# One signal for four message products, and one GpSimd wait for four gathered slots

## The chip, the cores and the metric

The kernel runs on one core of a Trainium2 chip. The metric is the device time of one launch in microseconds (us), as the median of several runs of the same program. The core has five engines that run at the same time and meet only through semaphores: TensorE (PE in the profile), VectorE (DVE), ScalarE (ACT), GpSimd (POOL) and SyncE (SP), which here only starts transfers.

## The reference, cut to what matters

A graph of 6250 nodes with 256 features and 200,000 edges, sorted by destination, goes through two graph convolutions, a linear attention block and a small mixture of experts:

```python
def _gcn_conv(x, edge_index, edge_weight, W, b):
    ...
    norm = dis[row] * ew * dis[col]
    h = x @ W.T
    msg = h[row] * norm[:, None]
    out = jax.ops.segment_sum(msg, col, num_segments=n)
    return out + b

def _block(x, edge_index, edge_weight, g, bln, W, b):
    h = _layer_norm(x, g, bln)
    h = _gcn_conv(h, edge_index, edge_weight, W, b)
    h = jax.nn.relu(h)
    return x + h
...
x = x + _L0_gnn_ref(xn, edge_index, edge_weight, ...) + _L0_mix_ref(xn[None], ...)[0]
x = x + _L0_ffn_ref(_layernorm(x, axis=-1)[None], ...)[0]
```

For each of the two convolutions every edge needs the row of its source node. The sum over the edges of a node is what the message products below compute.

## The kernel before, in words

The nodes are cut into 49 windows of 128 (`W`), the edges into 1563 chunks of 128 (`NCH`), 32 chunks to a window (`CH`). Each layer of the graph network goes once over the windows. The first layer's pass also computes the attention block of the same window, and the second layer's pass computes the eight experts, in fp16 halves.

A window uses 36 chunks (`USES`): its own 32 and two more at either side (`SIDE`). One use is one message product on TensorE (in `messages`): a 128x128 matrix `ss` that scatters 128 edges, times the 128x256 tile `gs` of gathered source rows, added up in PSUM bank 0 (`acc`). An fp32 product stands as two records in the trace. The products go in groups of four (`U`), one group `k` after the other with the window's other matmuls written out by hand between them (`window1`, `window2`).

Three engines feed this:
- GpSimd gathers a chunk with one indirect DMA into one of the 32 slots of `gs` (`gathers`, 3126 of them in two layers, written out one by one). Slot `n` of the next window may be overwritten once use `n + 2` of this window has been multiplied, so each gather waits on the semaphore `main_used`.
- VectorE builds the matrices `ss` four at a time into a ring of 18 (`scatter_group`, L1098). It waits on `main_used` too, for a value that lies in steps of four.
- TensorE waits on `main_set` for the `ss` of a group and on `main_in0` to `main_in31` for the gathered slots. Each product raises `main_used` by 1, and the last one of a short window by what is missing to 36. It starts at 18, the size of the ring.

TensorE raises many other semaphores, always attached to a matmul, in the order of its program. In a window of the first layer these are 11 beside the 36 of `main_used`: `self_used`, `xn1_tp`, `q_ps`, `nd_ps`, `z1_tp`, `msg_tp`, `h7_ps`, `m_ps`, `mn_tp`, `hh_ps`, `y1_ps`. In a window of the second layer they are 22: `hid_ps` and `y_ps` for each of eight experts, and `x2_tp`, `p_ps`, `z3_tp`, `g_ps`, `mt_ps`, `b2_ps`. After the fp16 matmuls of `hidden` raise `hid_ps`, ScalarE applies the gelu (L732) and copies (L735), VectorE makes the low half (L1222), and only then can TensorE do `expert_out` of that expert.

## Time and profile before

| | us |
|---|---|
| median of 3 runs | 5193.85 (5193.22 to 5195.35) |
| the profiled execution, its own time | 5195.25 |
| its span, first to last instruction | 5193.5 |
| TensorE busy | 3896.0 (75%) |
| GpSimd busy | 3080.2 (59%) |
| VectorE busy | 2524.4 (49%) |
| ScalarE busy | 1187.1 (23%) |

The span is shared by a preparation up to 261 us, the first layer's windows up to 2640 us, and the second layer's up to the end. Busy times are sums over the whole span; what a change is worth has to be read inside a window.

### The profile page before, as it was taken

Reading aid. Unit: us, or ns where it says so; the run is one execution under the profiler, and the core shown is the slowest. Engines: PE = TensorE matmul, PEld = TensorE weight load, DVE = VectorE, ACT = ScalarE, POOL = GpSimd, SP = SyncE. Lnnn points to the kernel's source line nnn. Section 1 sums busy time; section 2 is a strip of 40 time slices with the busy share of each in tenths; the row PEclk is TensorE's granted clock in tenths of the full one; section 3 lists DMA queues with packets and bytes.
Section 4 is the critical chain, followed back from the end, with each engine's and each line's share of the span. In section 5 each row is a group of like instructions: output and inputs, shape, how many; then the busy total and the mean of one; then the engine's idle time right before and its main releaser. Section 6 shows DMA issues by size and latency. Waiting matters only on the chain.

```text
span 5193.5 us, 89964 instructions
## 1 busy us (share of the span) xinstructions
PE 3896.0 (75%) x27204; PEld 3252.7 (63%) x27205; DVE 2524.4 (49%) x8946; ACT 1187.1 (23%) x3161; POOL 3080.2 (59%) x3315
## 2 busy tenths in 40 slices
PE   6847666766766766676658888888888888888888
PEld 4735555555555555555547777776777777777777
DVE  8734444444444444444434554454554554454554
ACT  3500000000000000000013333333333333333334
POOL 3266666666666666666645666666665666566662
PEclk9968877788888888888879999999999999999999
DMA  3333333333333333333323333333333333333331
GB/s 135 129 108 110 108 110 114 108 108 112 109 107 113 111 109 109 113 110 108 113 74 94 94 94 92 95 95 91 97 93 93 93 95 96 92 94 93 93 94 42
DMA packets 269256, 525.71 MB, mean 101 GB/s; under 512 B 62088, under 2 KB 168080, under 8 KB 269200
## 3 DMA queue, kind: packets, MB, share of 16 engines
q0 software_dynamic: 150144, 410.19, 27.0%
q1 hardware_dynamic: 119056, 114.93, 6.7%
q8 instruction: 16, 0.26, 0.0%
q14 instruction: 40, 0.33, 0.0%
HBM read 471.66 MB, written 53.22 MB: 101 GB/s over the span
## 4 chain that ended last, share of the span: by engine, by line
PE 31%; another core or an unknown queue 28%; issue 22%; ACT 10%; DVE 7%; SPq 1%; DVEq 1%; DMA 0%; ACTq 0%; POOL 0%; POOLq 0%
PE bank L1320 30%; ACT bank L732 5%; DVE ss L1098 2%; PE bank L1342 2%; ACT L732 1%; ACT L715 1%; ACT w L735 1%; DVE w L1222 1%; DVE rstd L752 1%; DVE rstd L751 0%; ACT hT L700 0%; DVE rstd L753 0%; DVE u L769 0%; DVEq L1098 0%
## 5 line engine op out<-in xcount | busy, mean ns | idle before, releaser
L571 POOL DMA_INDIRECT gs<-h_d,src_row x3126 | 2996.8, 959 | 1866.1 <-PE bank L1320 881.6
L1320 PE MATMUL bank<-gs,ss 128*128 128x256 f32 x7028 | 1857.2, 414 | 31.2 <-issue 15.2
L1320 PEld LDWEIGHTS bank<-gs,ss 128*128 128x128 f32 x7028 | 1431.2, 211 | 264.0 <-issue 55.3
L1098 DVE TENSOR_SCALAR ss<-iw,dst_all,ew_all 128x128 f32<-128x128 f32 x3514 | 988.8, 357 | 760.6 <-PE bank L1320 549.2
L1320 PE MATMUL bank<-experts,w 128*128 128x256 f16 x4848 | 605.8, 277 | 289.7 <-DVE w L1222 286.3
L1222 DVE SCALAR_TENSOR_TENSOR w<-bank,w 128x512 f16<-128x512 f32 x404 | 278.9, 690 | 1000.1 <-ACT w L735 923.8
L1320 PE MATMUL bank<-w,experts 128*128 128x128 f16 x9696 | 641.0, 220 | 126.1 <-issue 115.4
L732 ACT ACTIVATE bank<-bank,eb1c 128x128 f32<-128x128 f32 x1616 | 450.2, 341 | 1184.6 <-remote 1100.2
L1320 PEld LDWEIGHTS bank<-experts,w 128*128 128x128 f16 x4848 | 458.5, 99 | 391.3 <-issue 320.4
L1320 PEld LDWEIGHTS bank<-w,experts 128*128 128x128 f16 x9696 | 575.1, 98 | 185.5 <-issue 158.9
L1342 PE MATMUL bank<-ident,u 128*128 128x128 f32 x596 | 147.5, 336 | 497.6 <-DVE u L769 370.9
L1342 PEld LDWEIGHTS bank<-ident,u 128*128 128x128 f32 x596 | 81.4, 163 | 587.1 <-DVE u L769 389.3
L1216 DVE SCALAR_TENSOR_TENSOR u<-bank,mask_c,u 128x256 f32<-128x256 f32 x404 | 193.5, 479 | 106.9 <-PE bank L1320 86.7
L735 ACT ACTIVATE w<-bank 128x512 f16<-128x512 f32 x404 | 241.3, 597 | 12.8
L684 ACT ACTIVATE t_a<-t_a 128x256 f32<-128x256 f32 x49 | 20.4, 417 | 637.1 <-issue 470.8
L1320 PE MATMUL bank<-kvx,t_b 128*128 128x132 f32 x196 | 42.3, 347 | 144.6 <-issue 131.4
L1320 PE MATMUL bank<-xT,w 128*128 128x128 f32 x784 | 134.3, 299 | 17.9 <-ACT nT L696 10.2
L696 ACT COPY nT<-bank 128x256 f32<-128x256 f32 x49 | 18.2, 372 | 553.4 <-PE bank L1342 436.1
L700 ACT ACTIVATE hT<-bank,w1bias 128x128 f32<-128x128 f32 x196 | 56.0, 368 | 382.4 <-PE bank L1320 270.9
L1320 PEld LDWEIGHTS bank<-xT,w 128*128 128x128 f32 x784 | 124.5, 218 | 26.2 <-issue 19.7
L1320 PEld LDWEIGHTS bank<-kvx,t_b 128*128 128x128 f32 x196 | 31.1, 225 | 164.3 <-issue 149.1
L1320 PE MATMUL bank<-nT,w 128*128 128x128 f32 x784 | 127.2, 287 | 2.6 <-issue 2.6
(272 smaller groups left out, 3085.0 us busy)
## 6 DMA issues: line engine op xcount, KB each, us to landing
gs<-h_d,src_row POOLq DMA_INDIRECT x3126
hself<-self_d SPq DMA_DIRECT2D x100, 128.0 KB
ew_in<-in_eW SPq DMA_DIRECT2D x49, 168.0 KB
out<-u SPq DMA_DIRECT2D x51, 128.0 KB
u<-xn_d SPq DMA_DIRECT2D x50, 128.0 KB
h_d<-u SPq DMA_DIRECT2D x50, 128.0 KB
self_d<-u SPq DMA_DIRECT2D x50, 128.0 KB
u<-x_d SPq DMA_DIRECT2D x50, 128.0 KB
```

Source lines behind the costliest of these rows:

```text
L571: pool.indirect_dma_start(gs[:, n, :], None, table[:, :], bass.IndirectOffsetOnAxis(ap=src_row[:, c:c + 1], axis=0), element_offset=P * D) ...
L684: act.activation(t_a[1][:, :], t_a[0][:, :], ACT.Exp).then_inc(s["q_exp"], 1)
L700: act.activation(hT[0][:, j, :], bank[6][:, j * P:(j + 1) * P], ACT.Relu, bias=w1bias[:, j:j + 1]).then_inc(s["hr_done"], 1)
L715: act.copy(xT[:, :, :], half(1)).then_inc(s["x2T_set"], 1)
L732: act.activation(hid[e % 2][:, j, :], hid[e % 2][:, j, :], ACT.Gelu, scale=1.0 / (Z_UP * W_UP), bias=eb1c[:, e, j:j + 1]).then_inc(s["gelu ...
L735: act.activation(hT_part[e % 2][0][:, :, :], hid[e % 2], ACT.Copy, scale=H_UP).then_inc(s["h_high"], 1)
L752: ch.link(dve.tensor_tensor(t, t, minus_half, ALU.mult))
L1098: m = dve.tensor_scalar(ss[:, u % S_SLOTS, :], iw[:, :], dst_all[:, c], ew_all[:, c], ALU.is_equal, ALU.mult)
L1216: dve.scalar_tensor_tensor(out=u8[:, :], in0=wide((7, 5)[e % 2]), scalar=mask_c[:, e:e + 1], in1=u8[:, :], op0=ALU.mult, op1=ALU.add).then ...
L1222: dve.scalar_tensor_tensor(out=hT_part[e % 2][1][:, :, :], in0=hid[e % 2], scalar=H_UP, in1=hT_part[e % 2][0][:, :, :], op0=ALU.mult, op1= ...
L1320: return pe.matmul(out_ap, lhsT, rhs, start=first, stop=last, **kw)
L1342: m = pe.transpose(half(b)[:, k, :], src[:, k * P:(k + 1) * P], ident[:, :])
```

## The change

The four products of a group no longer raise `main_used` one by one: the last product of the group raises it by 4 (or by what is missing to 36). GpSimd waits for whole groups: a window's 32 gathers hold 9 waits where they held 32. VectorE's waits keep their values.

```diff
@@ -51,6 +51,7 @@
+assert SIDE < U and CH % U == 0
@@ -564,10 +565,10 @@
                     g, n = layer * W + c // CH, c % CH
-                    if n >= CH - SIDE:
-                        pool.wait_ge(s["main_used"], g * USES + (n - (CH - SIDE)) + 1 + S_SLOTS)
-                    elif g:
-                        pool.wait_ge(s["main_used"], (g - 1) * USES + n + SIDE + 1 + S_SLOTS)
+                    if n == CH - SIDE:
+                        pool.wait_ge(s["main_used"], g * USES + U + S_SLOTS)
+                    elif g and n < CH - SIDE and (n == 0 or (n + SIDE) % U == 0):
+                        pool.wait_ge(s["main_used"], (g - 1) * USES + (n + SIDE) // U * U + U + S_SLOTS)
@@ -1441,7 +1442,7 @@
                     m = mm(acc, ss[:, u % S_SLOTS, :], gs[:, n, :], layer == 1 and u == 0, True, skip_group_check=True)
-                    m.then_inc(s["main_used"], 1 if u + 1 < uses else USES - u)
+                m.then_inc(s["main_used"], U if k * U + U < uses else USES - k * U)
```

No instruction moves. On GpSimd, at the start of the first layer's gathers, the program before reads as follows (`table1` and `tab_set` belong to the preparation, `over_links` to a rare correction step, `table2` is the start of the second layer):

```order
L571 DMA gs<-h_d,src_row 128x256 [waits table1,tab_set]
L571 DMA gs<-h_d,src_row 128x256 x3
...
L571 DMA gs<-h_d,src_row 128x256 x26
L571 DMA gs<-h_d,src_row 128x256 [waits main_used] x1533
L571 DMA gs<-h_d,src_row 128x256 [waits main_used,table2]
```

The changed program has at the same place, for the chunks 4 to 49 of the first layer:

```order
L572 DMA gs<-h_d,src_row 128x256 x26
L572 DMA gs<-h_d,src_row 128x256 [waits main_used]
L572 DMA gs<-h_d,src_row 128x256
L572 DMA gs<-h_d,src_row 128x256 [waits main_used]
L572 DMA gs<-h_d,src_row 128x256
L572 DMA gs<-h_d,src_row 128x256 [waits main_used]
L572 DMA gs<-h_d,src_row 128x256 x3
L572 DMA gs<-h_d,src_row 128x256 [waits main_used]
L572 DMA gs<-h_d,src_row 128x256 x3
L572 DMA gs<-h_d,src_row 128x256 [waits main_used]
L572 DMA gs<-h_d,src_row 128x256 x3
```

The gathers are the same and in the same order, and the waits sit on the gathers themselves, so none of the rows that are gone was an instruction of its own. What a matmul signals is not printed in these rows; TensorE's rows are the same before and after.

## Rows read from the trace of the kernel before

**Rows 1.** The page: 40 slices of the span, and the costliest groups.

```profile
PEclk9968877788888888888879999999999999999999
POOL 3266666666666666666645666666665666566662
...
L571 POOL DMA_INDIRECT gs<-h_d,src_row x3126 | 2996.8, 959 | 1866.1 <-PE bank L1320 881.6
L1320 PE MATMUL bank<-gs,ss 128*128 128x256 f32 x7028 | 1857.2, 414 | 31.2 <-issue 15.2
```

**Rows 2.** Waits, whole span: engine, line, releaser: us in total, times, longest.

```profile
ACT bank L732 <- remote: 1100.2, 276, 29.1
DVE w L1222 <- ACT w L735: 923.8, 301, 33.3
POOL gs L571 <- PE bank L1320: 881.6, 802, 3.8
```

**Rows 3.** Timeline, window 0 of layer two, GpSimd: start, us, [idle before <-releaser].

```profile
2660.84 0.95 POOL L571 DMA_INDIRECT gs<-h_d,src_row  x1 [0.30 <-issue]
...
2697.18 0.94 POOL L571 DMA_INDIRECT gs<-h_d,src_row  x1 [0.30 <-issue]
2703.20 0.95 POOL L571 DMA_INDIRECT gs<-h_d,src_row  x1 [5.08 <-remote]
```

**Rows 4.** Timeline, where windows start on TensorE: two of each layer.

```profile
351.31 0.69 PE L1320 MATMUL bank<-hself,ident 128*128 128x256 f32 x2 [0.76 <-issue]
...
2607.60 0.70 PE L1320 MATMUL bank<-hself,ident 128*128 128x256 f32 x2 [0.67 <-DVE t_b L1163]
...
2746.35 1.99 PE L1320 MATMUL bank<-gs,ss 128*128 128x256 f32 x8
...
5111.22 1.92 PE L1320 MATMUL bank<-gs,ss 128*128 128x256 f32 x8
```

**Rows 5.** Timeline, a middle window of layer two, TensorE, ScalarE, GpSimd.

```profile
3506.86 1.50 PE L1320 MATMUL bank<-w,experts 128*128 128x128 f16 x24
3510.20 1.48 PE L1320 MATMUL bank<-experts,w 128*128 128x256 f16 x12 [1.84 <-DVE w L1222]
3511.52 1.89 PE L1320 MATMUL bank<-gs,ss 128*128 128x256 f32 x8
...
3513.68 1.12 ACT L732 ACTIVATE bank<-bank,eb1c 128x128 f32<-128x128 f32 x4 [4.33 <-remote]
...
3511.71 0.95 POOL L571 DMA_INDIRECT gs<-h_d,src_row  x1 [0.30 <-issue]
3514.11 0.95 POOL L571 DMA_INDIRECT gs<-h_d,src_row  x1 [1.46 <-PE bank L1320]
```

**Rows 6.** Timeline, the last window of layer two, all gathers done.

```profile
5106.02 0.95 POOL L571 DMA_INDIRECT gs<-h_d,src_row  x1 [2.16 <-PE bank L1320]
...
5117.18 1.50 PE L1320 MATMUL bank<-w,experts 128*128 128x128 f16 x24
...
5118.72 1.12 ACT L732 ACTIVATE bank<-bank,eb1c 128x128 f32<-128x128 f32 x4 [1.90 <-PE bank L1320]
...
5147.50 1.49 PE L1320 MATMUL bank<-experts,w 128*128 128x256 f16 x12 [0.77 <-DVE w L1222]
```

**Rows 7.** Timeline, window 0 of layer two, TensorE and ScalarE.

```profile
2669.41 0.63 PE L1342 MATMUL bank<-ident,u 128*128 128x128 f32 x2
2669.83 1.72 PE L1320 MATMUL bank<-w,experts 128*128 128x128 f16 x24
...
2670.07 0.37 ACT L715 COPY xT<-bank 128x256 f32<-128x256 f32 x1 [22.16 <-issue]
2700.84 1.12 ACT L732 ACTIVATE bank<-bank,eb1c 128x128 f32<-128x128 f32 x4 [29.09 <-remote]
```

**Rows 8.** Timeline, a middle window of layer one, TensorE, VectorE, GpSimd.

```profile
1466.14 0.72 PE L1320 MATMUL bank<-kvx,t_b 128*128 128x132 f32 x4 [2.66 <-issue]
...
1472.59 0.17 DVE L1135 TENSOR_SCALAR zden<-bank 128x8 f32<-128x8 f32 x1 [3.19 <-remote]
...
1472.67 0.95 POOL L571 DMA_INDIRECT gs<-h_d,src_row  x1 [2.17 <-remote]
```

## The prediction, as put on record before the change was run

> **What bounds the kernel now.** I read the page first: TensorE is busiest at 75%, but no slice of the 40 shows GpSimd above 0.6 or so, and the message products are 1857 us of TensorE while the gathers are 2997 us of GpSimd [rows 1]. No engine is full. So the question is who waits for whom, and the list of waits gives it: ScalarE's gelu waits 1100 us for something that the profile can't name ("remote"), VectorE's L1222 waits 924 us for that ScalarE, and the gathers wait 882 us for TensorE [rows 2].
>
> Next the timeline of one middle window of the second layer [rows 5]. TensorE's `hidden` of one expert starts at 3506.86 and has ended by 3508.36. ScalarE was idle and needs only its signal `hid_ps`, and yet starts at 3513.68, 5.3 us later. TensorE's group of message products starts at 3511.52, so its first product of 0.47 us (1.89 / 4) has ended by about 3512.0. GpSimd waits for that one from 3512.66 on (3511.71 + 0.95), and gets going at 3514.11. Both consumers wake within 0.4 us of each other, though what they wait for ended 3.6 us apart. That is how signals look that queue behind each other: TensorE's increments are seen late, and in order.
>
> The same view of the last window of the layer is the control. The last gather starts at 5106.02, and then GpSimd is silent. The same `hidden` runs from 5117.18 to 5118.68, and the gelu starts at 5118.72, after 0.04 us [rows 6]. From 5111.22 [rows 4] to that window's last `expert_out` at 5147.50 [rows 6] are 36.3 us, with seven full groups and a product of messages in it, where a middle window takes 50.3 us: (5111.22 - 2746.35) / 47 windows [rows 4].
>
> A third place tells what the lateness hangs on. At the start of layer two GpSimd streams 30 gathers without a pause, all of them free to go. The window's first signals get out: the flip at 2669.41 wakes ScalarE at 2670.07. The very next one, of the `hidden` that starts at 2669.83 and lasts 1.72 us, is seen at 2700.84, 29.3 us after its end, when GpSimd has run dry (2697.18 + 0.94) [rows 3, 7]. Layer one shows it too: the product for `nd_ps` ends at 1466.86, and VectorE sees it at 1472.59, together with GpSimd's own signal, at 1472.67 [rows 8]. My reading: while GpSimd works through gathers, only some half dozen of TensorE's increments get through; the rest wait until GpSimd pauses. Counted from the start of that stream, these are `over_used`, four of `main_used` and `x2_tp`: six, and `hid_ps` was the seventh. I infer this; no row names the mechanism.
>
> The loop that bounds a window is then: GpSimd streams the gathers it has leave for, TensorE's signals pile up, GpSimd runs out of leave and pauses, the signals get through, ScalarE, VectorE and TensorE move one step on, and GpSimd gets leave for the next few.
>
> **The floor.** 29 steps of the stream take 2697.18 - 2660.84 = 36.34 us, 1.253 us each [rows 3], so 32 gathers need 40.1 us. A window of layer one takes (2607.60 - 351.31) / 47 = 48.0 us, one of layer two 50.3 us [rows 4]. GpSimd thus pauses 7.9 us and 10.2 us per window.
>
> **The change part by part.** (1) The increments. It takes 27 of 36 off `main_used`. TensorE's increments per window go from 47 to 20 in layer one and from 58 to 31 in layer two (counted in the program). No instruction goes away and no matmul gets shorter, so on TensorE itself I cost this at nothing. On the loop it is everything: if the pauses serve to let increments through, they shrink with their number. Bounds: at one end nothing; at the other all pauses go. In between I take proportion, because the pauses of the two layers differ in the same sense as the counts (7.9 us for 47, 10.2 us for 58: 0.168 and 0.176 us per increment). Layer one gains 27 x 0.168 = 4.5 us a window, layer two 27 x 0.176 = 4.75 us. Over 47 windows each: 213 + 223 = 436 us.
>
> (2) The waits on GpSimd. 23 of 32 go. They were never instructions of their own, and the gathers' step is 1.253 us with satisfied waits [rows 3]; cost and gain nothing.
>
> (3) The later release. GpSimd now goes on when the fourth product has ended, not the first: 3 x 0.47 = 1.42 us later [rows 5]. Where TensorE's signals are late anyway this is covered: in [rows 5] the first product's signal is seen at about 3514.1 while the fourth had ended by 3513.40. Gathered rows are needed 30 or more uses later, so TensorE itself has most of a window in hand. I take 0, and up to 1.42 us for each wait that is answered promptly.
>
> (4) VectorE. Its values in steps of four used to be met by the second product of a group and are now met by the fourth, 0.94 us later, and its ring acts as one of 16. Behind the waiting instruction are the next step's operations: `hidden_low`, whose input comes from matmuls that TensorE does after that same group, or the layer norm, which waits for `m_ps` after the group too. So the wait is covered. If it weren't, 9 groups x 0.94 x 94 windows = 795 us would be the outer bound; I take nothing.
>
> Sum: 5195 (the profiled execution's own time, 1.4 above the median) - 436 = 4759, and 4758 against the median.
>
> **A rule of the Trainium skill beside this.** The page "TensorE: Matmul & The Clock Gate", section "The cost: per-tile semaphore tail", says that increments attached to matmuls serialise at 26.3 ns each and that one on the last matmul is enough. An estimate by it: 27 x 26.3 ns = 0.71 us a window, over 98 windows at most 70 us, so about 5125. The last window, where a signal came after 0.04 us, agrees that the tail is small when GpSimd is silent; the 29 us of the second layer's first window is nothing that this rule explains.
>
> **The rivals.**
> - *All pauses go.* With 20 or 31 increments for 32 gathers everything gets through in passing, and GpSimd becomes the bound. For it: the last window runs in 36.3 us, under the 40.1 us floor. Against it: the stream at 2660 to 2698 let nothing out for 28 us. Time: 5195 - 47 x (7.9 + 10.2) = 4344.
> - *Only the tail of the increments.* What is saved is a short service time per increment, hidden in most places. The nearest row is the prompt 0.04 us of [rows 6]; 27 x 0.04 x 94 = 100 us at most on the path, half of it likely: 5140. Speaking for it: [rows 5] has increments only a few per us. Against it: the 29 us wait.
> - *No change.* The lateness is the price of gathers in flight (their descriptors and transfers), however few the increments. Then the same six get through per pause in time, not in number, and the loop stays: 5195.
> - *Slower.* Lateness doesn't depend on the count, and the later release is paid where signals are prompt. GpSimd then begins each such stream 1.42 us later, and the next pause, which lets the signals out, comes later by as much. Two releases a window are enough to decide: 2 x 1.42 x 94 = 267 us, 5462. It decides from the point at which less than 1.42 us of lateness is left per group while GpSimd's stream still holds the loop. For it: GpSimd's waits are released by TensorE directly 802 times [rows 2]. Against it: in [rows 5] the fourth product was done before GpSimd saw the first.
>
> **How the numbers follow.** Proportion 0.45, all pauses go 0.20, only the tail 0.08, no change 0.07, slower 0.20. A measurement of this kernel can tell about 0.2% (10 us) from nothing. Faster 0.73, same 0.07, slower 0.20. The predicted time is that of the likeliest case, 4758; its own range, from pauses 1.5 times as much shortened to half as much, is 4540 to 4980. The whole range has to hold all but the larger part of the slower case: from 4330, just under the floor, to 5230.
>
> **What would show it.** Right: windows of 43.5 us and 45.6 us; the gelu's 1100 us of unnamed waits at least halved; a middle window's gelu within some 2 us of its `hidden`; GpSimd's pauses fewer, with runs of 8 gathers or more; the first window of layer two still held up, since nothing pauses there. GpSimd's busy share at 65% or more. Wrong, if the gelu still starts 4 to 5 us after its `hidden`: then the count of increments isn't the cause. Wrong to the slow side if the pauses before gathers grow by about 1.4 us. TensorE's granted clock, 0.7 to 0.8 in layer one [rows 1], may rise with shorter gaps; that would add to the gain and is not in the sum.

## The result, and the profile after

The changed kernel takes 5306.22 us (median of 4 runs, 5299.22 to 5322.39). On the same chip the kernel before takes 5194.6 us (4 runs, 5193.22 to 5197.19). The ratio is 1.0219, 95% interval 1.0195 to 1.0243: **2.2% slower**, where 4758 us and a gain were predicted. The profiled execution took 5322.39 us with a span of 5320.6 us, 127 us over the span of before, and 16 us above its own median.

The lines of the page and of the waits that answer to [rows 1, 2] (the lines of the program have moved down by one):

```profile
POOL 3266656666565566665646556565555555556552
PEclk9978878878888788887879999999999999999999
...
L572 POOL DMA_INDIRECT gs<-h_d,src_row x3126 | 2985.9, 955 | 2005.0 <-issue 778.9
L1321 PE MATMUL bank<-gs,ss 128*128 128x256 f32 x7028 | 1932.3, 420 | 181.2 <-issue 179.5
L1099 DVE TENSOR_SCALAR ss<-iw,dst_all,ew_all 128x128 f32<-128x128 f32 x3514 | 983.4, 353 | 1239.5 <-PE bank L1321 603.0
```

```profile
ACT bank L733 <- remote: 982.0, 286, 27.9
POOL gs L572 <- remote: 607.6, 367, 5.9
DVE ss L1099 <- PE bank L1321: 603.0, 153, 9.6
POOL gs L572 <- PE bank L1321: 551.6, 233, 6.1
DVE ss L1099 <- remote: 513.1, 177, 8.8
DVE w L1223 <- ACT w L736: 329.9, 110, 30.3
```

GpSimd's gathers are as long as before, but it idles 139 us more before them (2005.0 against 1866.1). TensorE now idles 181.2 us before message products, where it idled 31.2. The gelu still waits 982 us for something the profile can't name, where it waited 1100. VectorE's scatters have 513 us of such waits of their own now, where they had 154. The granted clock of TensorE did not rise (0.90 over the span in both).

Where windows start on TensorE, two of each layer, to be set beside [rows 4]:

```profile
351.95 0.69 PE L1321 MATMUL bank<-hself,ident 128*128 128x256 f32 x2 [0.76 <-DVE t_b L1164]
...
2696.79 0.70 PE L1321 MATMUL bank<-hself,ident 128*128 128x256 f32 x2 [0.68 <-DVE t_b L1164]
...
2832.48 1.99 PE L1321 MATMUL bank<-gs,ss 128*128 128x256 f32 x8
...
5238.41 1.91 PE L1321 MATMUL bank<-gs,ss 128*128 128x256 f32 x8
```

A window of layer one takes (2696.79 - 351.95) / 47 = 49.9 us (48.0 before), one of layer two (5238.41 - 2832.48) / 47 = 51.2 us (50.3 before). 47 x (1.88 + 0.87) = 129 us, which is all of the 127 us by which the span grew: the loss is a price per window, in both layers.

The timeline of a middle window of layer two, to be set beside [rows 5] (TensorE, GpSimd, ScalarE):

```profile
3509.76 0.94 POOL L572 DMA_INDIRECT gs<-h_d,src_row  x1 [0.30 <-issue]
3509.92 0.94 PE L1321 MATMUL bank<-w,experts 128*128 128x128 f16 x14
3511.75 0.72 PE L1321 MATMUL bank<-w,experts 128*128 128x128 f16 x10 [0.89 <-issue]
3512.27 0.94 POOL L572 DMA_INDIRECT gs<-h_d,src_row  x1 [1.56 <-remote]
...
3513.68 1.12 ACT L733 ACTIVATE bank<-bank,eb1c 128x128 f32<-128x128 f32 x4 [3.01 <-PE bank L1321]
```

`hidden` is 24 matmuls on data that are all there; TensorE does 14 of them and stops. GpSimd's last gather of its group ends at 3510.70, and TensorE's other 10 start at 3511.75. So TensorE is held up itself, not only its signals. A `hidden` torn like this, by more than 0.6 us, is found 174 times among 402 in the changed kernel, and 29 times in the kernel before (my count over the matmuls of both traces). So it is not new, only six times as frequent. The kernel before shows it at its strongest in the very stream of [rows 3, 7], which the prediction read for its signals only (TensorE, 4 of the 18 rows of one `hidden`):

```profile
2674.04 0.28 PE L1320 MATMUL bank<-w,experts 128*128 128x128 f16 x2
2675.47 0.22 PE L1320 MATMUL bank<-w,experts 128*128 128x128 f16 x1 [1.16 <-issue]
...
2694.53 0.27 PE L1320 MATMUL bank<-w,experts 128*128 128x128 f16 x1 [2.54 <-issue]
...
2702.93 0.60 PE L1320 MATMUL bank<-w,experts 128*128 128x128 f16 x4 [1.14 <-issue]
```

This is the `hidden` after the one whose signal is seen 29.3 us late. Its 24 matmuls, 1.5 us of work in [rows 5], take until 2703.53, mostly one or two at a time, with 0.4 to 2.5 us between them. TensorE crawls while the 30 gathers are issued.

In the changed kernel layer one shows the other form, the signal alone late:

```profile
1466.76 0.69 PE L1343 MATMUL bank<-ident,u 128*128 128x128 f32 x2 [2.99 <-DVE u L1140]
1467.50 0.95 POOL L572 DMA_INDIRECT gs<-h_d,src_row  x1 [0.30 <-issue]
1470.78 0.37 ACT L673 COPY zT<-bank 128x256 f32<-128x256 f32 x1 [7.91 <-remote]
1471.00 1.13 DVE L1099 TENSOR_SCALAR ss<-iw,dst_all,ew_all 128x128 f32<-128x128 f32 x4 [4.29 <-remote]
...
1471.11 0.94 POOL L572 DMA_INDIRECT gs<-h_d,src_row  x1 [2.66 <-remote]
```

The flip has ended by 1467.45, GpSimd's last gather by 1468.45, and then ScalarE, VectorE and GpSimd wake together between 1470.78 and 1471.11, 3.3 us after the flip. There are nine increments on `main_used` a window instead of 36, and the signals are still microseconds late.

From the starts of all gathers in the traces, one can count GpSimd's pauses (steps over 1.6 us) in the windows of each layer, and how far each goes beyond the step of 1.253 us:

```
                    layer one: pauses, beyond the step    layer two
kernel before        4.6 a window, 1.58 us each            8.0 a window, 1.23 us each
changed kernel       3.9 a window, 2.41 us each            8.0 a window, 1.37 us each
```

The pauses did not shrink. In layer one they are fewer and longer, and in sum 9.4 us a window in place of 7.3.

### The profile page after: what moved, and what is told of

It reads as the page before. It is cut to its first block, busy times and chain, and to the rows that moved or that the text cites. A ratio compares the mean times of both kernels' runs of the same rounds, so it can differ in the third digit from the quotient of the medians.

```text
span 5320.6 us, 90842 instructions
## 1 busy us (share of the span) xinstructions
PE 4024.5 (76%) x27204; PEld 3306.9 (62%) x27205; DVE 2532.6 (48%) x8946; ACT 1195.3 (22%) x3161; POOL 3069.1 (58%) x3315
## 3 DMA queue, kind: packets, MB, share of 16 engines
q0 software_dynamic: 150144, 410.19, 26.6%
## 4 chain that ended last, share of the span: by engine, by line
PE 47%; issue 21%; another core or an unknown queue 17%; DVE 8%; ACT 4%; SPq 1%; DVEq 1%; DMA 1%; ACTq 0%; POOL 0%; POOLq 0%
PE bank L1321 46%; DVE ss L1099 3%; PE bank L1343 1%; ACT bank L733 1%; ACT L733 1%; DVE w L1223 1%; DVE rstd L753 1%; DVE st L761 1%; ACT w L736 1%; DVEq L1099 1%; DVE rstd L754 1%; DVE rstd L752 0%; DVE t_c L770 0%; SPq L321 0%
## 5 line engine op out<-in xcount | busy, mean ns | idle before, releaser
L572 POOL DMA_INDIRECT gs<-h_d,src_row x3126 | 2985.9, 955 | 2005.0 <-issue 778.9
L1321 PE MATMUL bank<-gs,ss 128*128 128x256 f32 x7028 | 1932.3, 420 | 181.2 <-issue 179.5
L1321 PE MATMUL bank<-w,experts 128*128 128x128 f16 x9696 | 691.1, 219 | 293.8 <-issue 288.6
L1321 PE MATMUL bank<-w,zT 128*128 128x256 f32 x200 | 91.7, 606 | 131.4 <-ACT zT L673 131.4
L1321 PE MATMUL bank<-w,hT 128*128 128x256 f32 x392 | 148.5, 545 | 42.5 <-ACT hT L701 42.3
L1321 PEld LDWEIGHTS bank<-w,hT 128*128 128x128 f32 x392 | 103.3, 276 | 72.9 <-ACT hT L701 53.2
L1321 PEld LDWEIGHTS bank<-w,zT 128*128 128x128 f32 x200 | 53.4, 295 | 150.7 <-ACT zT L673 143.1
```

What stands on the lines that cost most here:

```text
L572: pool.indirect_dma_start(gs[:, n, :], None, table[:, :], bass.IndirectOffsetOnAxis(ap=src_row[:, c:c + 1], axis=0), element_offset=P * D) ...
L1321: return pe.matmul(out_ap, lhsT, rhs, start=first, stop=last, **kw)
```

## The experiments

Each kernel is compared with the kernel before on the same chip, since something came up with the first of them that the prediction had no way to see: **the kernel before is not equally fast on all chips.** On the chip of the result it takes 5195 us, on chips 7, 11 and 12 5144 to 5198 us, and on chips 8 and 14 4296 us. I call chips of the one kind late and of the other prompt; the reason for the words is in the first experiment. Which of the numbered chips the result came from isn't known. Late chips aren't steady either: chip 11 gave the kernel before 5144 us in one set of runs and 5196 us in another. The late times lie at two levels, 5144 and 5148 us (chips 11 and 12) and 5195 to 5198 us (the result's chip, chip 7, and chip 11 in its second set), so a cost of some tens of us can be trusted only within one set. The diffs below are cut to the lines that matter.

**1. Each half of the change alone, on a prompt chip (14).** First TensorE's half; GpSimd keeps its 32 waits.

```diff
-                    m.then_inc(s["main_used"], 1 if u + 1 < uses else USES - u)
+                m.then_inc(s["main_used"], U if k * U + U < uses else USES - k * U)
```

> The kernel before with one part of the change: the fourth product raises main_used by 4, but GpSimd keeps its 32 waits a window, with their old values, so that each is met by the end of its group. Theory A (what costs is that signals come only with the fourth product; how many waits GpSimd makes is nothing): as the changed kernel, 5306 us within 15. Theory B (GpSimd's own waits matter, few long ones are worse than many): clearly apart from it, near the 5195 us of before.

Then GpSimd's half; TensorE signals after every product.

```diff
-                    if n >= CH - SIDE:
-                        pool.wait_ge(s["main_used"], g * USES + (n - (CH - SIDE)) + 1 + S_SLOTS)
-                    elif g:
-                        pool.wait_ge(s["main_used"], (g - 1) * USES + n + SIDE + 1 + S_SLOTS)
+                    if n == CH - SIDE:
+                        pool.wait_ge(s["main_used"], g * USES + U + S_SLOTS)
+                    elif g and n < CH - SIDE and (n == 0 or (n + SIDE) % U == 0):
+                        pool.wait_ge(s["main_used"], (g - 1) * USES + (n + SIDE) // U * U + U + S_SLOTS)
```

> The kernel before with the other part: each product raises main_used by 1, but GpSimd waits once per group, for its fourth product. VectorE is released as before, by the second product of a group. Theory A1 (GpSimd's later release costs the time): 5290 to 5310 us. Theory A2 (VectorE's release by the fourth product instead of the second costs it): 5195 us within 15, and then the rest of the 111 us is VectorE's.

Measured: kernel before 4295.81 us (19 runs), TensorE's half 4305.17 us, ratio 1.0020 (1.0010 to 1.0029), GpSimd's half 4294.32 us, ratio 0.9999 (0.9989 to 1.0008). The second is as fast as the kernel before, so its trace stands here for that one on a prompt chip, of which there is no trace. Its timeline, a middle window of layer two, GpSimd, TensorE, ScalarE:

```profile
3027.22 0.95 POOL L571 DMA_INDIRECT gs<-h_d,src_row  x1 [0.30 <-PE bank L1320]
3028.23 1.50 PE L1320 MATMUL bank<-w,experts 128*128 128x128 f16 x24
3028.47 0.95 POOL L571 DMA_INDIRECT gs<-h_d,src_row  x1 [0.30 <-issue]
...
3029.72 0.94 POOL L571 DMA_INDIRECT gs<-h_d,src_row  x1 [0.30 <-issue]
3029.77 1.11 ACT L732 ACTIVATE bank<-bank,eb1c 128x128 f32<-128x128 f32 x4 [2.69 <-PE bank L1320]
3030.97 0.95 POOL L571 DMA_INDIRECT gs<-h_d,src_row  x1 [0.30 <-issue]
```

And its waits:

```profile
POOL gs L571 <- issue: 837.6, 2749, 0.3
...
ACT bank L732 <- PE bank L1320: 614.8, 298, 3.6
```

GpSimd streams without a pause, and the gelu starts 0.04 us after its `hidden` has ended (3028.23 + 1.50), in the middle of the stream. No wait is unnamed any more. The windows' medians are 40.8 us in layer one and 40.1 us in layer two, GpSimd's 32 steps of 1.253 us. This is the prediction's rival "all pauses go", within 1.2% of its 4344 us, reached by another chip and not by the change.

**2. The whole change on a prompt chip (8).** The changed kernel as it is.

> The changed kernel itself, timed again beside the kernel before, because in the first experiments the kernel before took 4296 us where it had taken 5195 us. If the kernel before takes 4296 us again: both parts alone cost 9 us and nothing there, so I expect a ratio of 1.000 to 1.004. If the kernel before takes 5195 us: a ratio of 1.0195 to 1.0243, as first measured.

Measured: 4307.05 us against 4296.17 us, ratio 1.0024 (1.0014 to 1.0035): TensorE's half and nothing more.

**3. Without gathers, on both kinds of chip (14, then 7).** In place of the gathers GpSimd only sets their semaphores; the buffers are filled with zeros once.

```diff
-                    pool.indirect_dma_start(
-                        gs[:, n, :], None, table[:, :],
-                        bass.IndirectOffsetOnAxis(ap=src_row[:, c:c + 1], axis=0),
-                        element_offset=P * D).then_inc(s[f"main_in{n}"], 16)
+                    pool.sem_inc(s[f"main_in{n}"], 16)
```

> The kernel before without the gathers: gs is filled with zeros once, and GpSimd only raises main_in by 16 where it would have started a gather; all waits stay. So the message sums are of zeros; nothing else is left out. My reading that TensorE's signals are late because GpSimd works through gathers: windows fall to 36 to 38 us in both layers, the gelu follows its hidden by under 0.3 us, and the time is 5195 - 94 x 12.5 = 4020 us, 3950 to 4150. The rival (TensorE is late for a reason of its own, its queue or its clock): windows stay above 45 us, over 4900 us.

> The gathers left out (the message products are of zeros), only their semaphores set by GpSimd. It took 3955 us on a chip with prompt signals. Theory A (the gathers are what holds up TensorE's signals): 3950 to 3970 us on any chip, also on one where the kernel before takes 5150 us. Theory B (that chip's TensorE signals are late by themselves): 4300 us or more there, with ScalarE starting microseconds after its matmul.

Measured: 3955.39 us on chip 14 and 3953.35 us on chip 7, where the kernel before takes 5197.93 us. The waits on chip 7:

```profile
ACT bank L732 <- PE bank L1320: 631.2, 304, 3.6
...
DVE ss L1098 <- PE bank L1320: 380.3, 237, 4.2
```

Without gathers there is one kind of chip only. The late chip's TensorE, its signals and its other engines are then as quick as the other's, and not one `hidden` is torn. What the gathers cost is 340 us on a prompt chip and 1245 us on a late one (one run of each kernel without gathers).

**4. Gathers paced by their landing (14).** Each gather also waits until the one before its predecessor has landed.

```diff
+                    if c >= 2:
+                        pool.wait_ge(s[f"main_in{(c - 2) % CH}"], 16 * (layer * -(-(NCH - (c - 2) % CH) // CH) + (c - 2) // CH + 1))
```

> The kernel before, in which each gather also waits until the gather two before it has landed, so that at most two are in flight. If lateness comes from a backlog of gathers in flight, TensorE's signals come sooner after their matmul and the windows get shorter in spite of slower gathers, unless two gathers take over 3 us to land (then GpSimd's step of over 1.5 us makes windows of over 48 us, and the time is above 5195). If it comes from GpSimd's own work on a gather, the lateness stays at 3 to 5 us wherever its step stays near 1.25 us. The median step of the gathers gives their time to land.

Measured: 5964.59 us, one run. Two gathers now take about 3.6 us together (a layer's windows of 32 take 57.3 and 57.9 us), so that is about the time from a gather's start to its landing. It says that transfers must overlap and, on a prompt chip, nothing on the lateness.

**5. How much of a gather is needed (late chip 7).** The same instruction, with only 2 or 64 of the 128 rows.

```diff
-                        gs[:, n, :], None, table[:, :],
-                        bass.IndirectOffsetOnAxis(ap=src_row[:, c:c + 1], axis=0),
+                        gs[0:2, n, :], None, table[:, :],
+                        bass.IndirectOffsetOnAxis(ap=src_row[0:2, c:c + 1], axis=0),
```

> Each gather fetches two rows of 1 KB in place of 128 (the other 126 partitions of the buffers hold zeros, so the message sums miss their terms). Theory G (GpSimd's own work on the instruction holds up TensorE): a gather still takes GpSimd some 0.9 us, pauses stay, and the time on a chip that holds up signals stays above 4900 us. Theory T (the rows' transfers or their descriptors do it): under 4150 us on every chip, near the 3955 us without gathers. On a chip with prompt signals: 3955 to 4300 us, and it says only what a gather of two rows costs GpSimd.

> Each gather fetches 64 of the 128 rows (the other partitions hold zeros). Theory G: GpSimd's step shortens only if its work goes by rows; if it stays at 1.25 us, 5000 to 5200 us on a chip that holds up signals. Theory T: half the price, 4400 to 4750 us there. On a chip with prompt signals: 3955 us if the step falls below 1.05 us, 4296 us if it stays.

Measured, one run each: two rows 5337.16 us, 64 rows 5325.06 us, the kernel before 5197.93 us there. The page of the kernel with two rows:

```profile
GB/s 131 128 19 24 22 24 26 23 21 26 24 21 25 25 21 24 26 22 22 26 19 13 10 12 10 12 13 9 13 10 12 10 12 13 9 13 10 12 10 14
...
q0 software_dynamic: 100128, 7.04, 1.3%
...
L574 POOL DMA_INDIRECT gs<-h_d,src_row x3126 | 2750.7, 880 | 2218.6 <-PE bank L1323 1211.3
...
L735 ACT ACTIVATE bank<-bank,eb1c 128x128 f32<-128x128 f32 x1616 | 448.7, 341 | 1192.4 <-remote 1102.6
```

The transfers are all but gone (9 to 26 GB/s from the third slice on, where the kernel before moves about 100), GpSimd's instruction still takes 880 ns in place of 959, and the gelu's unnamed waits are 1103 us, as in [rows 2]. So the rows on their way don't make the chip late; what GpSimd does to issue the gather does, or what stays of it on the DMA side. Something does stay there: by the page, the queue of the gathers carries 100128 packets in place of 150144, though they take 1.3% of the DMA engines' time in place of 27.0%. Work per packet is thus not excluded. That both are slower than the whole gather, by 2.7% and 2.4%, I had not expected. GpSimd's step is shorter, 1.17 and 1.21 us, and the pauses longer by more than that.

**6. GpSimd as busy, but without gathers (late chip 11).** Instead of each gather GpSimd fills a scratch tile.

```diff
-                    pool.indirect_dma_start(
-                        gs[:, n, :], None, table[:, :],
-                        bass.IndirectOffsetOnAxis(ap=src_row[:, c:c + 1], axis=0),
-                        element_offset=P * D).then_inc(s[f"main_in{n}"], 16)
+                    pool.wait_ge(s["breath"], layer * NCH + c)
+                    pool.memset(breath[:, :], 0.0).then_inc(s["breath"], 1)
+                    pool.sem_inc(s[f"main_in{n}"], 16)
```

> In place of each gather GpSimd fills a scratch tile of 128x1024 (about 0.9 us, after the same wait for the slot), and then sets the gather's semaphore (the message products are of zeros). GpSimd is so about as busy as with gathers, and issues none. Theory A (only the issuing of gathers holds TensorE's signals): 3955 to 4100 us also on a chip that holds them up, TensorE's signals prompt. Theory B (GpSimd being busy holds them): 4900 us and more there. On a chip with prompt signals 3955 to 4100 us by both.

Measured, one run: 4327.59 us, the kernel before 5196.36 us there. Its page:

```profile
L575 POOL MEMSET breath<- 128x1024 f32 x3126 | 2986.2, 955 | 972.1 <-PE bank L1322 601.1
L1100 DVE TENSOR_SCALAR ss<-iw,dst_all,ew_all 128x128 f32<-128x128 f32 x3514 | 1570.3, 717 | 348.5 <-PE bank L1322 320.6
...
L734 ACT ACTIVATE bank<-bank,eb1c 128x128 f32<-128x128 f32 x1616 | 448.8, 340 | 631.6 <-PE bank L1322 631.0
```

GpSimd is busy for 955 ns at a time, as with gathers, and the gelu's waits are 632 us and named, as without gathers. The time is above the expected range, most likely because VectorE's scatters take 717 ns in place of the 342 ns that they take without gathers (not isolated). TensorE isn't held: not one `hidden` is torn. A GpSimd that is busy as long doesn't hold TensorE up; issuing gathers does.

**7. The change taken apart, on late chips.** On chip 11, first VectorE's later release by itself (TensorE and GpSimd as before):

```diff
-                dve.wait_ge(s["main_used"], v + k * U + U)
+                dve.wait_ge(s["main_used"], v + k * U + U + 2)
```

> The kernel before with one edit: VectorE waits, before each group of four scatters, for two message products more than it needs (the released count in its wait is raised by 2), so that it builds the matrices as late as the changed kernel lets it; TensorE still signals after each product and GpSimd still waits for single products. On two chips the TensorE part of the change alone cost 9.4 us and the whole change 10.9 us of 4296. Theory A (VectorE's later release is the whole price of the change where signals are not held up): the ratio comes out at 1.002, 4304 to 4308 us, with layer one's windows at 41.0 instead of 40.8 us and layer two's unchanged at 40.1. Theory B (the price is on GpSimd's side or in TensorE's own stream, one signal of four in place of four): ratio 1.000 within 0.0007, and windows as before. Should this chip hold up the signals as the one where the kernel before took 5194 us did, A gives 5270 to 5310 us (most of the 112 us that the change cost there), B 5190 to 5200.

Second, the changed kernel with VectorE released as early as before: the signal of four is split into two of two.

```diff
+                    if u % U == 1 and u + 1 < min(k * U + U, uses):
+                        m.then_inc(s["main_used"], 2)
-                m.then_inc(s["main_used"], U if k * U + U < uses else USES - k * U)
+                m.then_inc(s["main_used"], U - 2 if k * U + U < uses else USES - k * U - (2 if uses - k * U > 2 else 0))
```

> The changed kernel with one edit: TensorE signals 2 after the second product of each group and 2 after the fourth, in place of 4 after the fourth. VectorE, whose waits are met by the second product, is so released as early as in the kernel before, and GpSimd still waits once per group of four. Theory A (VectorE's later release is the price): ratio 1.000 within 0.001, 4294 to 4299 us, so 9 to 11 us under the changed kernel. Theory B (GpSimd's group waits and the late release of its buffers are the price): ratio 1.002, about 4306 us. Should this chip hold up the signals as the first one did, A gives 5180 to 5205 us or less, B about 5300.

Third, TensorE's half alone, the kernel of experiment 1:

> The TensorE part of the change alone again, beside the two kernels above on one chip: one signal of four after the last product of a group, with GpSimd's 32 single waits per window kept. Theory A: 4304 to 4308 us, equal to the kernel with VectorE's waits raised by two within 3 us. Theory B as well, but then above that kernel by some 9 us. Should this chip hold up the signals, this run says how much of the 112 us that the change cost there is TensorE's part: all of it (5300 us) by A, less than half (under 5250 us) if GpSimd's group waits carry the loss.

Measured on chip 11, kernel before 5143.95 us (9 runs):

```
VectorE released two products later   5181.42 us   1.0074 (1.0054 to 1.0094)   +37 us
pairs of signals, GpSimd in groups    5173.31 us   1.0050 (1.0032 to 1.0068)   +29 us
one signal of four                    5206.05 us   1.0120 (1.0099 to 1.0141)   +62 us
```

Neither theory holds alone. VectorE's share is 37 us taken by itself, and 33 us as the difference of the last two rows, which differ in GpSimd's waits and in the number of signals too. The other 29 us stay when VectorE is released early, and I put them down to GpSimd, which gets its buffers back after the fourth product. The two parts, each measured by itself, add up to 66 us, where 62 us were measured together.

On chip 12, GpSimd's half and the whole change:

> Only the GpSimd part of the change: one wait per group of four slots; TensorE signals after each product. On a chip that takes signals promptly this was 1.000. On a chip that holds them up: theory A (the loss is TensorE's single signal and VectorE's late release) gives 0.998 to 1.002 of the kernel before; theory B (GpSimd's group waits add to the pauses as well, which would make up the difference between the 62 us that the TensorE part cost on one such chip and the 112 us of the whole change on another) gives 1.006 to 1.012, 30 to 60 us more.

> The changed kernel beside its GpSimd part on the same chip. Where signals are prompt, 1.002 (4305 to 4308 us). Where they are held up: theory A gives 1.012, as the TensorE part alone did; theory B 1.018 to 1.024, the sum of both parts.

Measured, kernel before 5147.93 us (7 runs): GpSimd's half 5214.33 us, ratio 1.0112 (1.0087 to 1.0137); the whole change 5203.66 us, ratio 1.0113 (1.0095 to 1.0131). What costs nothing on a prompt chip costs 66 us here. The whole change costs no more there than its GpSimd half, 1.1%, and 2.2% where the result was taken; why the price doubles stays open. So does why GpSimd's half costs 66 us here, when pairs of signals with the same groups on GpSimd cost 29 us on chip 11: chip and number of signals both differ. The kernel before stood at the lower of the two late levels in both sets of this experiment (5144 and 5148 us) and at the upper one at the result (5195 us), so the 112 us themselves were not taken apart. Groups of eight, too, cost more at the upper level (experiment 8).

**8. Larger groups on GpSimd.** The kernel before with a wait once per 8 slots, and once per 16; TensorE and VectorE as before.

```diff
-                    if n >= CH - SIDE:
-                        pool.wait_ge(s["main_used"], g * USES + (n - (CH - SIDE)) + 1 + S_SLOTS)
-                    elif g:
-                        pool.wait_ge(s["main_used"], (g - 1) * USES + n + SIDE + 1 + S_SLOTS)
+                    if n == CH - SIDE:
+                        pool.wait_ge(s["main_used"], g * USES + U + S_SLOTS)
+                    elif g and n < CH - SIDE and (n == 0 or (n + SIDE) % 8 == 0):
+                        pool.wait_ge(s["main_used"], (g - 1) * USES + (n + SIDE) // 8 * 8 + 8 + S_SLOTS)
```

> The kernel before, with GpSimd waiting once per eight slots of the ring (5 waits a window in place of 32), TensorE and VectorE as before. On the chips that hold up signals a window was 40.1 us of gathers and about 8 pauses of GpSimd of 1.1 to 1.4 us in layer two, 4 to 5 of 1.6 us in layer one. Theory A (a pause has a fixed price and their number is set by the groups that GpSimd waits in): pauses halve in layer two, window 45 to 46.5 us in place of 50, total 4900 to 5050 us there. Theory B (TensorE needs a given time without gathers for each window's signals, however it is cut): pauses half as many and twice as long, total 5130 to 5200 us; with longer streams holding up the chain of the experts, up to 5300 us. Where signals are prompt: no wait for a slot binds and the time stays within 0.3% of the kernel before.

> As before but once per sixteen slots (3 waits a window). Theory A: 2 to 3 pauses a window, 43 to 44 us in layer two, total 4750 to 4950 us where signals are held up. Theory B: 5130 to 5400 us. Where signals are prompt: GpSimd may now run out of free slots, since 16 of the 32 have to be free at once: 4296 to 4400 us.

> The kernel before with GpSimd waiting once per eight slots. On a chip with held-up signals it cost 13.8%: 1.138 again within 0.01. On a chip with prompt signals, theory A (only held-up signals make long groups dear): within 0.3% of the kernel before, 4285 to 4310 us. Theory B (late release of eight slots alone starves the products): 4400 us and more.

Measured: groups of eight 5852.08 us on chip 12, ratio 1.138 (1.136 to 1.140), and 6008.39 us on chip 7, ratio 1.156 (1.154 to 1.158); groups of sixteen 6460.28 us on chip 12, ratio 1.253 (1.250 to 1.256). The timeline of a middle window of layer two with groups of eight, GpSimd, TensorE, ScalarE:

```profile
3834.78 0.97 POOL L571 DMA_INDIRECT gs<-h_d,src_row  x1 [9.19 <-PE bank L1320]
...
3839.30 1.52 PE L1320 MATMUL bank<-w,experts 128*128 128x128 f16 x21
...
3841.87 0.33 PE L1320 MATMUL bank<-w,experts 128*128 128x128 f16 x3 [1.04 <-issue]
...
3843.56 0.94 POOL L571 DMA_INDIRECT gs<-h_d,src_row  x1 [0.30 <-issue]
3846.41 1.12 ACT L732 ACTIVATE bank<-bank,eb1c 128x128 f32<-128x128 f32 x4 [7.50 <-remote]
3850.76 1.50 PE L1320 MATMUL bank<-w,experts 128*128 128x128 f16 x24
3851.08 0.95 POOL L571 DMA_INDIRECT gs<-h_d,src_row  x1 [6.58 <-PE bank L1320]
```

Eight gathers run in one go from 3834.78 to 3844.50. TensorE stops within a `hidden` meanwhile and goes on at 3841.87, still within the run of gathers; its signal is seen at 3846.41, and GpSimd then waits 6.6 us until TensorE has used eight slots. Over layer two there are 5.0 pauses a window, 4.6 us each beyond the step, and with sixteen 2.0 pauses of 15.8 us. Both theories had half as many pauses, for the same total or less; neither had them nearly four times as long. Every step from single waits to groups of four, eight and sixteen is slower than the one before on chip 12: 5148, 5214, 5852, 6460 us. No prompt chip ran groups of eight or sixteen. So the rival of the last run's expectation stands untested: that handing back eight slots at once starves the products by itself, whatever holds TensorE.

**9. A short gap after each gather (late chip 11).** The kernel before with a fill of a 128x256 tile behind each gather.

```diff
+                    pool.wait_ge(s["breath"], layer * NCH + c)
+                    pool.memset(breath[:, :], 0.0).then_inc(s["breath"], 1)
```

> The kernel before with a fill of a 128x256 scratch tile (about 0.3 us) and a wait for it after each gather, so that a gather's step is about 1.65 us in place of 1.25 us: 32 of them are 53 us. Theory A (a gap of half a microsecond lets TensorE's signals through): no further pauses, windows at GpSimd's 53 us, 5450 to 5600 us on every chip, ScalarE starting at once after its matmul. Theory B (only a gap of some 1 us does): the pauses of 8 to 10 us a window come on top, 5850 us and more where signals are held up; 5450 to 5600 us where they are not.

Measured: 5238.2 us against 5196.36 us, ratio 1.0071 (1.0050 to 1.0091). The step is 1.44 us, not the 1.65 us that I had taken, so 32 of them are 46.2 us. The page:

```profile
L571 POOL DMA_INDIRECT gs<-h_d,src_row x3126 | 2995.4, 958 | 890.1 <-issue 436.3
...
L576 POOL MEMSET breath<- 128x256 f32 x3126 | 1040.4, 333 | 1.6
...
L734 ACT ACTIVATE bank<-bank,eb1c 128x128 f32<-128x128 f32 x1616 | 448.8, 341 | 1152.5 <-remote 1116.8
```

It came out between the theories. GpSimd does 1040 us more work and the kernel is only 42 us slower: the fills mostly take the place of pauses. The gelu's unnamed waits are as before, so a gap of 0.5 us between gathers does not bring the gelu's signals in time. It helps in part: `hidden` is torn by more than 0.6 us twice in 402, not 29 times, and more signals get out during gathers (the table below).

## Why the prediction was wrong

**The reading of the bound held, on the kind of chip that it was read from.** The loop of gathers, late signals and pauses is there. Gathers make TensorE late (experiment 3), by their issuing and not by the transfer of their rows or by GpSimd's busy time (5 and 6). The floor was right too: 40.1 us a window, met by layer two on chips 8 and 14 (layer one took 40.8 to 40.9 us there). What I had inferred from one stream, that TensorE is the engine concerned, can be counted. The trace holds the times at which semaphores were raised. The share of each engine's signals that fall into a gather's (or, in the sixth experiment, a fill's) busy time should be GpSimd's share of that stretch, if the two have nothing to do with each other (my count over those times, for semaphores that one engine alone raises):

```
                              GpSimd busy   TensorE's   VectorE's   ScalarE's
kernel before, late chip         0.62         0.31        0.56        0.64
changed kernel, late chip        0.60         0.29        0.58        0.61
two rows a gather, late chip     0.55         0.24        0.53        0.64
gap after gathers, late chip     0.61         0.48        0.68        0.78
fills for gathers, late chip     0.75         0.72        0.69        0.82
GpSimd's half, prompt chip       0.75         0.74        0.72        0.77
```

On a late chip half of TensorE's signals that should fall into a gather fall behind it; VectorE's and ScalarE's show no such lack, and the changed kernel is no different in this. One reservation: where gathers run on a late chip, the trace holds 93% of TensorE's signals (kernel before), but 70% of VectorE's and 69% of ScalarE's. On prompt chips, and without gathers, it holds all. So for those two engines the table speaks for the recorded signals only. Nor is TensorE held throughout: in the kernel before, 0.61 of its matmuls start within a gather, as chance would have it.

**Step (1), the increments, is what failed: "if the pauses serve to let increments through, they shrink with their number".** They don't. With 27 fewer increments a window the pauses grew from 7.3 to 9.4 us (layer one) and from 9.9 to 11.0 us (layer two). The text gave as its own test that the gelu might still start 4 to 5 us after its `hidden`, and then the count isn't the cause. In layer one the flip of 1466.76 is seen 3.3 us after its end. In layer two the gelu starts 1.2 us after the end of its `hidden` (3511.75 + 0.72), only because `hidden` itself is torn in two and late. The half dozen signals that got out at the start of the stream were counted as signals; what the runs show is time. TensorE's signals are held while gathers are being issued, and at times its matmuls too; in the changed kernel the torn rows of `hidden` go on 1.04 us after the end of the last gather (median), and the flip's signal of layer one is seen 2.3 us after it. The crawl from 2674.04 to 2703.53 stood in the trace of the kernel before and was a hint that more than a queue of signals was at stake, since TensorE stops there between matmuls of one row, of which only the last has a signal to give. That 47 and 58 increments went with pauses of 7.9 and 10.2 us was a coincidence of two points, and two points can't carry a proportion. The 436 us of gain were worth nothing.

**Step (2), GpSimd's fewer waits at 0: right as a cost of the instructions.** The step stays 1.25 us. But the same edit is step (3).

**Step (3), the later release at 0: wrong on late chips.** It was taken as covered since the fourth product had ended before GpSimd saw the first. GpSimd's half alone costs 66 us on chip 12, and I put 29 us of TensorE's 62 on chip 11 down to the same. The ends that I compared were those of a trace in which GpSimd was already pausing. My reading, argued and not isolated: a group released as one lets the next stream start later and hold TensorE for four gathers at once. The torn rows of `hidden` fit it. They are 29 in the kernel before and 31 when only VectorE is released later (chip 11); where GpSimd is released by groups they are 73 (GpSimd's half, chip 12), 117 (TensorE's half, chip 11), and 118 and 174 (the whole change, chip 12 and the result's chip). So do the groups of eight and sixteen, at 1.138 and 1.253, unless the late release of so many slots costs this by itself. On prompt chips the 0 was right (0.9999).

**Step (4), VectorE's later release at 0: wrong, small.** It costs 33 to 37 us on a late chip, far from its outer bound of 795 us. On a prompt chip TensorE's half, which includes it, costs 9 us, mostly in layer one's windows (40.95 us, against 40.79 us with GpSimd's half, medians); whether it is VectorE's part there wasn't tried.

**The rivals.** The rival "slower" had the mechanism: lateness that doesn't depend on the count, and a release paid where it is waited for. Its price was too high, 2.84 us a window where 112 / 94 = 1.2 us was paid, so 5462 against 5306 us. It had 0.20 and should have been the forecast, since the profile had evidence for lateness by gathers and none for lateness by count. "No change" had transfers in flight as its cause, and with 2 of 128 rows the lateness stays. The support that "all pauses go" had from the last window was thinner than it looked: its 36.3 us end at the start of the last `expert_out`, which lasts 1.49 us more, and it has 7 products fewer than a full window. "Only the tail of the increments" has nothing left either. The Trainium skill's page "TensorE: Matmul & The Clock Gate", section "The cost: per-tile semaphore tail", has increments serialise at 26.3 ns, which was an estimate of up to 70 us of gain here. TensorE's half on the prompt chip, where nothing else is in the way, came out at +9 us, so no run here shows that saving. It need not be at odds with the rule, as TensorE isn't the bound of those windows.

**What stays open.** Why issuing a gather holds TensorE on some chips and not on others; through what, GpSimd's own work or the packets of the gather; what groups of eight cost on a prompt chip; and why the chip of the result pays 2.2% and chip 12 1.1% for the same kernel. No version was found that beats the kernel before on either kind.

## What to carry to other kernels

When signals are late, ask first what goes on during the lateness, and remove that (here the gathers) or vary it, before counting what is late; two layers that agree in a ratio are no test of it. A release in larger groups is free only where its waiter has slack: where a loop runs through that signal, it is paid at every turn, and here steeply as groups grew (1.00, 1.01, 1.14, 1.25 for groups of one, four, eight and sixteen on chip 12). Read a stall on every engine that could take part in it: the signals looked late, and the matmuls in the same rows were late too. And if a profile has large waits without a name, take the kernel to another chip first: here it ran 17% faster, unchanged, and the change that was to win 436 of those 900 us won none of them.

## What was unexpected of the hardware

- The same program takes 5144 to 5198 us on chips 7, 11, 12 and that of the result, and 4296 us on chips 8 and 14, and 3953 to 3955 us on one of each kind (7 and 14, one run each) once its gathers are left out.
- On late chips TensorE stops within a row of ready matmuls while GpSimd issues gathers, and starts again about 1.0 us after the last one (3510.70 to 3511.75), or crawls on within a long stream (24 matmuls in 29.5 us from 2674.04, 1.5 us elsewhere); its signals wait likewise. A gather of 2 rows does this as well as one of 128 (44 and 29 torn rows of 402), a fill of equal length doesn't (none).
- On late chips the profile loses records of signals while gathers run: it holds 4114 of VectorE's 5843 in the kernel before, and all of them on a prompt chip or without gathers.
- GpSimd's time for a gather hardly goes by its rows: 880 ns for 2, 924 ns for 64, 959 ns for 128.
- Fills of 955 ns on GpSimd take VectorE's scatters from 342 to 717 ns. The Trainium skill's page "SBUF — State Buffer", section "SBUF: two separate sides", describes a pair of ports that VectorE, in its modes that use both of its ports, and GpSimd lock against each other for a whole instruction. The scatters' longer time fits it, if they run in such a mode, which no run here shows. With gathers they take 354 ns (GpSimd's half, prompt chip).
